# Two attention layers and two feed-forward layers in one kernel: the last expert's rows by a product, the fold earlier, three batches with the plain context

## The chip, the cores and the metric

One core of one Trainium2 chip runs the whole program. The metric is the device time of one execution in microseconds, the median of the runs. Everything is in float32 except a few small bfloat16 helpers.

## The reference

`x` has 8 batches of 112 rows and 256 columns, the context 8 batches of 375 rows. Four residual stages follow one another:

```python
x = x + L0_xattn(layernorm(x), ctx)      # 16 heads
x = x + L0_moe(layernorm(x))             # 8 experts of 112 slots each, top 1
x = x + L1_xattn(layernorm(x), ctx)      # one head of width 256, scores / sqrt(16)
x = x + L1_ffn(layernorm(x))             # 1024 hidden, plus rank-one terms from rows of x
```

In the expert stage each row goes to the expert with the largest gate; its slot is the expert's number times 112 plus its rank among the rows of that expert, and rows past 112 are dropped. The row gets back its gate times the expert's output at its slot. In the second attention the value is `v = ctx @ Wv + bv`, and the result `softmax(...) @ v`. Because the probabilities of a row sum to one, `softmax @ (ctx @ Wv) = (softmax @ ctx) @ Wv`, and `bv` is added to the residual separately.

## The kernel before

The tensor engine's program is written out in the order in which it runs; the other engines follow by semaphores. Each engine runs its own list strictly in order. Products go to one of 8 banks of PSUM; `open_bank` makes the tensor engine wait until every earlier product of that bank has been read (`drained`), `full` makes the reader wait until it is written (`filled`). Where it does not matter which bank is used, `next_bank` goes round a list by one counter; `CTX_BANKS` is (2, 3, 6, 7).

1. **First attention** (to about 172 us). `PIPE` and, for the last batches, `LAST` give for each step `(i, u)` the small pieces that run beside the scores: C1 to C6 and D5, D6 are the output projection, the norm and the router of one batch; ND, NM the row maxima. "CV" with a number means so many chunks of `project_context`: one chunk is 125 rows of the context times `Wv` of the second attention, two matmuls of 256 columns, and the scalar engine copies it to `ctxV` (L964). There are 24 chunks (3 for each batch); they depend on nothing that is late, so they are put wherever the tensor engine would wait.
2. **Experts** (L645 to L685). GpSimd has scattered each batch's rows to DRAM by slot (L1417), and SP has loaded them back by expert. `expert_rows` transposes the rows of an expert (bank 6 or 7), `expert_up` makes the 1024 hidden values, `expert_down` the output (bank 4 or 5). VectorE adds `b2` to the output (L1253) and SP stores it to `eo_dram` (L1535); the buffers are `eo0` and `cc` in turn. 7 chunks stand before the first expert, one behind the first up product.
3. **Behind the experts** (L690 to L711). The tensor engine makes the fold `Wq Wk^T` of the second attention (`WQK`, L695, 4 matmuls of 256 columns), a chunk, the products of the biases (`WQKB`, L704 and L707), and four chunks. Meanwhile GpSimd waits until the outputs of all 8 experts are in DRAM, and gathers each batch's rows from there (L1442, 8 indirect DMAs). VectorE's `combine` (L1268) waits for the gathered rows of a batch, adds gate times rows to the residual (L1271) and takes the moments for the norm (L1105 to L1107); GpSimd makes the inverse root (L1372), VectorE normalises (L1111).
4. **Second attention** (loop over `i`, `attend(stage, b)` with `b = i - stage`). Stage 0 transposes the normalised rows (XT3), 1 multiplies by the fold (QK), 2 makes the scores (S1), 3 transposes the probabilities (PT), 4 multiplies them by `ctxV` (O1), 5 transposes the rows for the last stage (XT4). The two last chunks stand at `i` = 0 and `i` = 1 (`CTX_IN_SECOND`). VectorE in each `i`: the norms, the combines (batches 1 and 2 at `i` = 0, then `i` + 2), then stages 4 and 2.
5. **Last feed-forward**, from `i` = 9 on, to the end at 352.8 us.

Of the kernel before, what the change touches and what calls it, by code (L numbers as in the profile page):

```python
# [6 lines left out]
ALU = mybir.AluOpType  # L7
# [105 lines left out]
CTX_AFTER_FIRST_UP = 1  # L113
CTX_BEHIND_FOLD = 1
CTX_IN_SECOND = {0: 1, 1: 1}
CTX_BANKS = (2, 3, 6, 7)

# [68 lines left out]
def build(nc, A):  # L186
    out = A["out"]
    with ExitStack() as ctx:
# [60 lines left out]
        wv_at1 = w_in[:, 0]  # L249

        unread = sb("unread", [1, 1])
        vones = [sb(f"vones{n}", [P, NKC, H, VW]) for n in range(2)]
        ctxU = sb("ctxU", [P, 4 * S])
        cc = sb("cc", [S, D])
# [22 lines left out]
        idx_get = sb("idx_get", [S, NB], I32)  # L277

# [9 lines left out]
        wqk = cut(late, DT * D).rearrange("p (k e) -> p k e", k=DT)  # L288
# [3 lines left out]
        tq = [cut(late, 1) for _ in range(2)]  # L292

# [44 lines left out]
        ld_wv_at1 = sem("loaded_at1_wv")  # L338
        ld_ring = [sem(f"loaded_expert{n}") for n in range(RING)]
# [47 lines left out]
        def _(pe):  # L387
# [161 lines left out]
            def project_context(n, banks):  # L549

                for _ in range(n):
                    t = chunks_done[0]
# [11 lines left out]
            def post(stage, b):  # L564
                if stage == "CV":
                    project_context(b, spare)
                elif stage in ("P0", "P1", "P2"):
                    weighted(b, int(stage[1]))
                elif stage in ("V0", "V1", "V2"):
# [105 lines left out]
            for e in range(E + 1):  # L675
# [7 lines left out]
                if e == 0:  # L683
                    project_context(CTX_AFTER_FIRST_UP, (5,))
# [6 lines left out]
            pe.wait_ge(ld["at1w"], 32)  # L691
            o = open_bank("WQK", 0)
            for m in range(DT):
                for k in range(DT):
                    mm = pe.matmul(o[:, m * D:(m + 1) * D], w_at1[:, 0, k, m * P:(m + 1) * P], w_at1[:, 1, k, :],  # L695
                                   start=k == 0, stop=k == DT - 1)
            mm.then_inc(filled[0], 1)
            project_context(CTX_BEHIND_FOLD, CTX_BANKS)
# [11 lines left out]

            project_context(NB * NKC - chunks_done[0] - sum(CTX_IN_SECOND.values()), CTX_BANKS)  # L711

            def attend(stage, b):
# [26 lines left out]
                elif stage == 3:  # L740
# [5 lines left out]
                    mm.then_inc(filled[4], 1)  # L746
                elif stage == 4:
# [4 lines left out]
                    for c in range(NKC):  # L752
                        mm = pe.matmul(o[0:S, 0:D], pT1[s][0:KC, c, :], ctxV[0:KC, NKC * b + c, :],  # L753
                                       start=c == 0, stop=c == NKC - 1)
                    mm.then_inc(filled[6], 1)
# [61 lines left out]
            for i in range(FFN_STEPS):  # L817
                for stage in (4, 2, 3, 1, 0):
                    if 0 <= i - stage < NB:
                        attend(stage, i - stage)  # L820
# [810 lines left out]
```

## Time and profile before

| | |
|---|---|
| median of 3 runs (lowest to highest) | 355.02 us (355.02 to 355.38) |
| the profiled execution's own time | 354.55 us |
| its span, first to last instruction | 352.8 us |
| PE (tensor engine, matmul) busy | 341.8 us, 97% |
| PEld (its weight loads, beside the matmuls) | 261.5 us, 74% |
| DVE (VectorE) / ACT (ScalarE) / POOL (GpSimd) busy | 189.2 / 146.1 / 57.7 us |
| granted TensorE clock | 1.000 |

The engine times overlap, so they are no sum. Each float32 matmul stands in the trace as two LDWEIGHTS and two MATMUL instructions; "x8" at L695 are the 4 matmuls of the fold. A "start us" is counted from the span's start. In the timeline the bracket behind a row says how long the engine had stood idle and who released it; the durations of matmuls in it overlap a little, so the pace of a row of matmuls is read from the chain, where they are laid end to end.

### The profile page before, as it was taken

What the parts mean: (1) busy time and instruction counts of PE and PEld (TensorE: products, weight loads), DVE (VectorE), ACT (ScalarE), POOL (GpSimd) and SP (SyncE); (2) the same over time, 40 slices, a digit from 0 to 9 for tenths busy, and PEclk for the clock granted to TensorE, in tenths of its full rate; (3) what the DMA queues carried; (4) which work ended last, traced back from release to release, by engine and by line L of the source; (5) the groups of instructions that cost most, each with busy time, mean ns of one, the idle gap of its engine ahead of it and who ended that gap; (6) DMA issues with size and microseconds to landing.
All of it is one profiled execution on the core that took longest, in us unless ns stands there. A gap on an engine that the chain in (4) does not pass through costs nothing.

```text
span 352.8 us, 7953 instructions
## 1 busy us (share of the span) xinstructions
PE 341.8 (97%) x3128; PEld 261.5 (74%) x3128; DVE 189.2 (54%) x591; ACT 146.1 (41%) x340; POOL 57.7 (16%) x95
## 2 busy tenths in 40 slices
PE   7999999999999999997999999999899999999996
PEld 6546566666666666665889998988688889797875
DVE  4674668857675867755721121212987667351500
ACT  2437353646365545554431221112446675332400
POOL 3200204101010010101200000134865211200000
DMA  8984150700001000062074999811110101101000
GB/s 234 336 260 159 32 208 5 251 4 13 3 9 37 2 15 3 16 238 76 20 216 142 323 339 331 238 40 52 39 28 3 44 16 54 55 27 52 29 26 26
DMA packets 24884, 35.28 MB, mean 100 GB/s; under 512 B 2608, under 2 KB 21408, under 8 KB 24736
## 3 DMA queue, kind: packets, MB, share of 16 engines
q1 hardware_dynamic: 22160, 31.73, 28.0%
q0 software_dynamic: 768, 1.84, 1.7%
q10 hardware_dynamic: 1920, 1.21, 1.3%
q8 instruction: 25, 0.41, 0.5%
q14 instruction: 11, 0.09, 0.1%
HBM read 31.06 MB, written 3.72 MB: 99 GB/s over the span
## 4 chain that ended last, share of the span: by engine, by line
PE 85%; DVE 6%; issue 3%; ACT 3%; POOL 2%; DMA 1%; DVEq 0%; POOLq 0%; ACTq 0%; SPq 0%
PE ps L661 8%; PE ps L806 8%; PE ps L671 8%; PE ps L784 7%; PE ps L424 6%; PE ps L497 6%; PE ps L517 5%; PE ps L452 5%; PE ps L560 4%; PE ps L538 4%; PE ps L737 3%; PE ps L512 2%; PE ps L608 2%; PE ps L753 2%; PE ps L415 2%
## 5 line engine op out<-in xcount | busy, mean ns | idle before, releaser
L1143 DVE TENSOR_REDUCE mneg<-ps 112x2 f32<-112x750 f32 x64 | 56.9, 932 | 19.2 <-PE ps L497 19.2
L1372 POOL TENSOR_TENSOR rstd<-veps,neghalf 112x1 f32<-112x1 f32 x32 | 18.6, 582 | 98.3 <-DVE veps L1107 97.4
L924 ACT ACTIVATE heads<-ps 125x896 f32<-125x896 f32 x34 | 29.3, 915 | 12.5 <-PE ps L517 12.5
L497 PE MATMUL ps<-heads 32*112 32x375 f32 x256 | 30.8, 519 | 0.1
L661 PEld LDWEIGHTS ps<-xT,ring 128*128 128x128 f32 x256 | 29.8, 192 | 1.1 <-ACT xT L877 0.7
L661 PE MATMUL ps<-xT,ring 128*128 128x112 f32 x256 | 29.9, 275 | 0.4 <-ACT xT L877 0.4
L806 PE MATMUL ps<-heads,ring 128*112 128x256 f32 x128 | 28.8, 382 | 0.0
L671 PE MATMUL ps<-ring,heads 128*112 128x256 f32 x128 | 28.8, 379 | 0.0
L806 PEld LDWEIGHTS ps<-heads,ring 128*112 128x112 f32 x128 | 22.4, 177 | 6.1 <-issue 1.4
L452 PE MATMUL ps<-w_in,ctxT 128*125 128x256 f32 x96 | 26.5, 402 | 0.0
L517 PE MATMUL ps<-heads 32*125 32x224 f32 x384 | 25.6, 354 | 0.0
L671 PEld LDWEIGHTS ps<-ring,heads 128*112 128x112 f32 x128 | 22.1, 177 | 4.4
L784 PE MATMUL ps<-xT,heads 128*128 128x224 f32 x128 | 24.9, 353 | 0.0
L1260 DVE TENSOR_SCALAR heads<-ps,b1col 128x112 f32<-128x112 f32 x32 | 8.6, 327 | 29.3 <-PE ps L661 29.3
L784 PEld LDWEIGHTS ps<-xT,heads 128*128 128x128 f32 x128 | 24.0, 190 | 0.1
L424 PE MATMUL ps<-ctxT,w_in 128*128 128x375 f32 x64 | 23.7, 492 | 0.2 <-ACT vones L907 0.2
L560 PE MATMUL ps<-w_in,ctxT 128*125 128x256 f32 x96 | 23.4, 385 | 0.0
L452 PEld LDWEIGHTS ps<-w_in,ctxT 128*125 128x125 f32 x96 | 16.2, 187 | 8.9 <-issue 6.3
L981 ACT ACTIVATE heads<-ps,b1col 128x112 f32<-128x112 f32 x32 | 8.7, 354 | 33.1 <-PE ps L661 33.1
L1312 DVE SCALAR_TENSOR_TENSOR ring<-ring,xT,ps 128x112 f32<-128x112 f32 x64 | 16.9, 326 | 8.5 <-PE ps L784 8.5
L1051 ACT ACTIVATE ring<-ring,fb1col 128x224 f32<-128x224 f32 x32 | 13.6, 474 | 19.0 <-DVEq L1317 18.9
L1417 POOL DMA_INDIRECT expert_in_dram<-xn,idx_put x8 | 8.0, 996 | 77.9 <-DVE idx_put L1219 77.9
(150 smaller groups left out, 552.8 us busy)
## 6 DMA issues: line engine op xcount, KB each, us to landing
ring<-in_L_ffn_W SPq DMA_DIRECT2D x16, 1024.0 KB, 6.3
ctxT<-in_ctxT SPq DMA_DIRECT2D x8, 375.0 KB, 11.5
heads<-in_L_ffn_W SPq DMA_DIRECT2D x2, 1024.0 KB, 9.4
ring<-x_by_odd_rows_dram SPq DMA_DIRECT2D x4, 448.0 KB, 3.7
ring<-in_mask SPq DMA_DIRECT2D x1, 1312.5 KB, 7.1
expert_in_dram<-eo SPq DMA_DIRECT2D x1, 896.0 KB, 11.0
b2row<-in_L_ffn_b SPq DMA_DIRECT2D x8, 112.0 KB, 7.4
out_dram<-ring SPq DMA_DIRECT2D x8, 112.0 KB, 1.9
```

The costliest lines, as they stand in the source:

```text
L424: mm = pe.matmul(o[:, 0:S2], w_in[:, 1, k, m * P:(m + 1) * P], ctxT[:, k, b * S2:(b + 1) * S2], start=k == 0, stop=k == DT - 1)
L452: mm = pe.matmul(o[0:KC, 0:D], ctxT[:, k, b * S2 + c * KC:b * S2 + (c + 1) * KC], w_in[:, 2, k, :], start=k == 0, stop=k == DT - 1)
L497: mm = pe.matmul(tile(("MX", b, g), j)[0:S, 0:S2], qz[rows, m, a, b * S:(b + 1) * S], kt[b % 3][rows, m, :], start=True, stop=True)
L517: mm = pe.matmul(tile(key, j)[0:KC, x * QW:(x + 1) * QW].rearrange("p (a q) -> p a q", a=2), kt[b % 3][rows, m, c * KC:(c + 1) * KC], qz[r ...
L560: mm = pe.matmul(o[0:KC, 0:D], ctxT[:, k, b * S2 + c * KC:b * S2 + (c + 1) * KC], wv_at1[:, k, :], start=k == 0, stop=k == DT - 1)
L661: mm = pe.matmul(o[:, f * S:(f + 1) * S], w1e[e % RING][:, k, ft * P:(ft + 1) * P], xT[:, k, e * S:(e + 1) * S], start=k == 0, stop=k == D ...
L671: mm = pe.matmul(o[0:S, 0:D], hid[e % 2][:, ft, :], w2e[e % RING][:, ft, :], start=ft == 0, stop=ft == FT - 1)
L784: mm = pe.matmul(o[:, f * 2 * S:(f + 1) * 2 * S], w1f[:, k, ft * P:(ft + 1) * P], xT[:, k, 2 * p * S:2 * (p + 1) * S], start=k == 0, stop= ...
L806: pe.matmul(o[0:S, 0:D], gT[p % 2][:, ft, x * S:(x + 1) * S], w2f[:, ft, :], start=ft == 0, stop=False)
L924: act.activation(weights(b, step)[0:KC, js.start:js.stop, :], o[0:KC, :, 0:2 * QW], ACT.Exp, scale=DK ** -0.5).then_inc(free, 1)
L1143: v.tensor_reduce(mneg[:, b % 2, PAIRS * g + js.start:PAIRS * g + js.stop], o[0:S, :, 0:S2], AX.X, ALU.max, negate=True).then_inc(free, 1)
L1372: g.tensor_tensor(rstd[:, b:b + 1], veps[:, b:b + 1], neghalf[:, b:b + 1], ALU.pow)\
```

## The change

Three things, all in one step.

**The last expert's rows by a product.** For batches 0 to 2 (`BY_PRODUCT`) VectorE builds a 112 by 112 matrix of ones and zeros from the rows' slots (`at_slot`: row's slot equals 784 + column). The tensor engine transposes it behind the rows of experts 1, 2 and 3, ScalarE copies it (`from_slot`), and behind the last expert's output three products `ER` (banks 4, 6, 7) pick the rows from the output still on chip (`cc`). The gathers of these batches read only experts 0 to 6 (rows of the last expert get index 0 and gate 0) and wait only for those stores. `combine` of these batches adds twice: the gathered rows, then the product. The gathers of batches 3 to 7 are issued one by one behind the roots of batches 0 to 4.

**The fold ahead of the experts.** `WQK` becomes a stage "FW" at step (8, 3), in place of two of the three chunks there; its result goes to a weight buffer that is free by then.

**Three batches weigh the plain context.** For batches 3, 4, 5 (`RAW`) the chunks are not made; SP loads their context rows as they are into `ctxV` (1.1 MB, behind the weights of expert 2). Stage 4 then makes `(softmax @ ctx)` transposed (PC, bank 7, 6 matmuls of 112 columns), ScalarE copies it (`pcT`) and at the end of the same `i` a product with `Wv` (WV, 2 matmuls of 256 columns) fills O1. VectorE takes stage 2 ahead of stage 4 for them. Of 24 chunks 15 are left: 9 go away, namely the one at (6, 1), two at (8, 3), the one behind the first up product, and all five behind the experts. Those at `i` = 0 and 1 stay.

```diff
-    (6, 1): [("C2", 5), ("CV", 1), ("C6", 4), ("D6", 4)],
+    (6, 1): [("C2", 5), ("C6", 4), ("D6", 4)],
-    (8, 3): [("CV", 3), ("L2", 7), ("D6", 6)],
+    (8, 3): [("FW", 0), ("CV", 1), ("L2", 7), ("D6", 6)],
...
@@ tensor engine
+                elif stage == "FW":
+                    pe.wait_ge(ld["at1w"], 32)
+                    n = next_bank(spare)
+                    o = open_bank("WQK", n)
+                    ... (the four matmuls that stood behind the experts)
...
             def expert_rows(e):
                 n = 6 + e % 2
                 pe.wait_ge(xe_loaded[PART_OF[e]], 16)
-                transpose_x("XE", e, n)
+                o = open_bank(("XE", e), n)
+                for k in range(DT):
+                    mm = pe.transpose(o[:, k * S:(k + 1) * S], xn[:, e, k * P:(k + 1) * P], ident[0:S, 0:S])
+                if 1 <= e <= BY_PRODUCT:
+                    pe.wait_ge(at_slot_ready, e)
+                    mm = pe.transpose(o[0:S, DT * S:(DT + 1) * S], at_slot[e - 1], ident[0:S, 0:S])
+                mm.then_inc(filled[n], 1)
...
-                if e == 0:
-                    project_context(CTX_AFTER_FIRST_UP, (5,))
...
-            (fold), project_context(CTX_BEHIND_FOLD, CTX_BANKS)
+            for b in range(BY_PRODUCT):
+                if b == 0:
+                    read(("DN", E - 1))
+                read(("XE", b + 1))
+                n = (4, 6, 7)[b]
+                pe.matmul(open_bank(("ER", b), n)[0:S, 0:D], from_slot[b], eo[(E - 1) % 2][:, :], start=True, stop=True)\
+                  .then_inc(filled[n], 1)
...
-            project_context(NB * NKC - chunks_done[0] - sum(CTX_IN_SECOND.values()), CTX_BANKS)
+            project_context(len(CTX_CHUNKS) - chunks_done[0] - sum(CTX_IN_SECOND.values()), CTX_BANKS)
...
+                elif stage == 4 and b in RAW:
+                    pe.wait_ge(ld_raw, 16)
+                    read(("PT", b))
+                    o = open_bank(("PC", b), 7)
+                    for m in range(DT):
+                        for c in range(NKC):
+                            mm = pe.matmul(o[:, m * S:(m + 1) * S], ctxV[0:KC, NKC * b + c, m * P:(m + 1) * P],
+                                           pT1[s][0:KC, c, :], start=c == 0, stop=c == NKC - 1)
+                    mm.then_inc(filled[7], 1)
...
+                elif stage == "WV":
+                    read(("PC", b))
+                    o = open_bank(("O1", b), 6)
+                    for k in range(DT):
+                        mm = pe.matmul(o[0:S, 0:D], pcT[:, k, :], wv_at1[:, k, :], start=k == 0, stop=k == DT - 1)
...
@@ VectorE
+            v.wait_ge(slot_row_ready, 1)
+            step(v.tensor_copy(slot_of[:, :], idx_get[:, 0:BY_PRODUCT]))
+            step(v.tensor_scalar(in_others[:, :], slot_of[:, :], float(LAST_SLOT), None, ALU.is_lt))
+            v.tensor_tensor(gate_others[:, :], gate[:, 0:BY_PRODUCT], in_others[:, :], ALU.mult)
+            v.tensor_tensor(idx_others[:, :], slot_of[:, :], in_others[:, :], ALU.mult).then_inc(others_ready, 1)
+            for b in range(BY_PRODUCT):
+                v.tensor_scalar(at_slot[b], slot_row, slot_of[:, b:b + 1], None, ALU.is_equal).then_inc(at_slot_ready, 1)
...
-                step(v.scalar_tensor_tensor(xres[:, b, :], xn[:, b, :], gate[:, b:b + 1], xres[:, b, :],
+                weight = gate_others if b < BY_PRODUCT else gate
+                step(v.scalar_tensor_tensor(xres[:, b, :], xn[:, b, :], weight[:, b:b + 1], xres[:, b, :],
                                             ALU.mult, ALU.add))
+                if b < BY_PRODUCT:
+                    o, free = full(("ER", b))
+                    v.scalar_tensor_tensor(xres[:, b, :], o[0:S, 0:D], gate[:, b:b + 1], xres[:, b, :],
+                                           ALU.mult, ALU.add).then_inc(free, 1)
+                    drained_by_me(("ER", b))
...
-                for stage in (4, 2):
+                for stage in (2, 4) if i - 4 in RAW else (4, 2):
...
@@ GpSimd
+            g.wait_ge(eo_stored[0], 16 * (E // 2))
+            g.wait_ge(eo_stored[1], 16 * (E // 2 - 1))
+            g.wait_ge(others_ready, 1)
+            for b in range(BY_PRODUCT):
+                gather(b, idx_others, LAST_SLOT)
+            for i in range(GATHER_AHEAD, NB + GATHER_AHEAD):
+                root(3, i - GATHER_AHEAD)
+                if i == GATHER_AHEAD:
+                    g.wait_ge(eo_stored[1], 16 * (E // 2))
+                if i + 1 < NB:
+                    gather(i + 1, idx_get, T)
...
@@ SP, behind the loads of experts 0 to 2
+            sp.dma_start(ctxV[0:KC, NKC * RAW[0]:NKC * (RAW[-1] + 1), :],
+                         A["ctx"][:, NKC * RAW[0]:NKC * (RAW[-1] + 1), :]).then_inc(ld_raw, 16)
```

## Rows read from the trace of the kernel before

**Rows 1.** Chain that ended last, in order of time: start us, us, what.

```profile
173.15 6.16 PE ps L560 x28
...
188.60 0.19 PE ps L415 x2
188.79 3.46 PE ps L671 x16
...
261.52 0.89 PE ps L727 x8
...
262.97 1.30 PE ps L753 x6
```

**Rows 2.** Timeline, 138 to 147: start us, us, engine line op out<-in, count [idle before <-releaser].

```profile
138.98 1.78 DVE L1143 TENSOR_REDUCE mneg<-ps 112x2 f32<-112x750 f32 x2 [0.24 <-PE ps L497]
...
142.50 0.42 DVE L1183 TENSOR_TENSOR xres<-ps,xres 112x256 f32<-112x256 f32 x1 [0.40 <-PE ps L608]
...
146.30 0.11 PEld L584 LDWEIGHTS ps<-identb,mpieces 112*128 112x128 bf16 x2 [0.28 <-DVE mpieces L1157]
```

**Rows 3.** DMA issues by line: KB each, median us to landing.

```profile
heads<-in_L_xattn_Wk SPq DMA_DIRECT2D x1, 256.0 KB, 3.8
```

**Rows 4.** Timeline, 159 to 170, the fold's weights and the chunks of (8, 3).

```profile
159.29 0.47 SPq L1516 DMA_DIRECT2D heads<-in_L_xattn_Wk  x1
...
167.43 2.83 PE L560 MATMUL ps<-w_in,ctxT 128*125 128x256 f32 x12
```

**Rows 5.** Timeline, 183.8 to 189, behind the first expert's up product.

```profile
183.81 0.36 PE L415 MATMUL ps<-ident,xn 112*128 112x112 f32 x2
...
184.20 0.36 ACT L877 ACTIVATE xT<-ps 128x224 f32<-128x224 f32 x1 [0.89 <-PE ps L415]
...
184.88 3.72 PE L661 MATMUL ps<-xT,ring 128*128 128x112 f32 x32
```

**Rows 6.** Busy time by stretch, with counts (x), granted clock (PEclk), DMA share, GB/s.

```profile
180.00:238.80 58.80, 58.66 (x403) 53.65 (x404) 11.55 (x40) 11.67 (x41) 3.90 (x8) 1.00 0.74 238
238.80:251.80 13.00, 11.94 (x72) 10.11 (x70) 6.45 (x20) 4.94 (x15) 7.55 (x9) 1.00 0.18 53
...
262.00:285.00 23.00, 23.00 (x155) 18.44 (x155) 17.20 (x54) 13.93 (x45) 8.76 (x15) 1.00 0.08 23
```

**Rows 7.** Timeline, 235 to 252, behind the experts.

```profile
235.83 0.31 SPq L1535 DMA_DIRECT2D expert_out_dram<-eo  x1
...
238.79 0.42 DVE L1253 TENSOR_TENSOR cc<-ps,b2row 112x256 f32<-112x256 f32 x1 [3.03 <-PE ps L671]
239.29 0.30 SPq L1535 DMA_DIRECT2D expert_out_dram<-cc  x1
...
241.18 1.84 PE L704 MATMUL ps<-bcol,heads 128*128 128x1 f32 x16
...
241.93 0.99 POOL L1442 DMA_INDIRECT xn<-expert_out_dram,idx_get  x1 [9.61 <-DMA expert_out_dram<-cc]
...
244.66 0.48 DVE L1271 SCALAR_TENSOR_TENSOR xres<-xn,gate,xres 112x256 f32<-112x256 f32 x1 [5.44 <-DMA xn<-expert_out_dram,idx_get]
...
246.70 0.41 DVE L1111 TENSOR_SCALAR xn<-xres,mv,rstd 112x256 f32<-112x256 f32 x1 [0.69 <-POOL rstd L1372]
...
247.03 0.48 DVE L1271 SCALAR_TENSOR_TENSOR xres<-xn,gate,xres 112x256 f32<-112x256 f32 x1
...
247.17 0.41 PE L415 MATMUL ps<-ident,xn 112*128 112x112 f32 x2 [0.20 <-DVE xn L1111]
...
248.29 0.47 DVE L1271 SCALAR_TENSOR_TENSOR xres<-xn,gate,xres 112x256 f32<-112x256 f32 x1
...
249.55 0.40 DVE L1111 TENSOR_SCALAR xn<-xres,mv,rstd 112x256 f32<-112x256 f32 x1
...
250.26 1.04 PE L560 MATMUL ps<-w_in,ctxT 128*125 128x256 f32 x4
...
251.86 1.49 PE L737 MATMUL ps<-ctxT,ring 128*112 128x375 f32 x4 [0.56 <-ACT ctxV L964]
```

More of the change, by code:

```diff
@@ L112 @@
 CTX_BEFORE_EXPERTS = 7
-CTX_AFTER_FIRST_UP = 1
-CTX_BEHIND_FOLD = 1
 CTX_IN_SECOND = {0: 1, 1: 1}
 CTX_BANKS = (2, 3, 6, 7)
+RAW = (3, 4, 5)
+CTX_CHUNKS = [NKC * b + c for b in range(NB) if b not in RAW for c in range(NKC)]
+BY_PRODUCT = 3
+LAST_SLOT = (E - 1) * CAP
 ROW_PARTS = ((0, 1), (1, 2), (2, 4), (4, E))
@@ L253, in build @@
         ctxU = sb("ctxU", [P, 4 * S])
+        slot_row = vones[0][0:S, 0, :, :].rearrange("p h w -> p (h w)")[:, 0:S]
+        at_slot = [vones[1][0:S, b, :, :].rearrange("p h w -> p (h w)")[:, 0:S] for b in range(BY_PRODUCT)]
+        from_slot = [ctxU[0:S, b * S:(b + 1) * S] for b in range(BY_PRODUCT)]
         cc = sb("cc", [S, D])
@@ L971, in _ @@
                         copy_context_values(b)
+                    elif stage == "FW":
+                        o, free = full("WQK")
+                        act.activation(wqk, o[:, 0:DT * D].rearrange("p (k e) -> p k e", k=DT), ACT.Copy)\
+                           .then_inc(free, 1)
                     elif stage in ("V0", "V1", "V2", "K0", "K1", "QX", "Q0", "Q1", "U", "C2", "C4", "D5"):
@@ L991, in _ @@
                 if e + 1 < E:
+                    if e < BY_PRODUCT:
+                        o, _ = full(("XE", e + 1))
+                        act.activation(from_slot[e], o[0:S, DT * S:(DT + 1) * S], ACT.Copy)
                     copy_xT("XE", e + 1)
-                if e == 0:
-                    copy_context_values(CTX_AFTER_FIRST_UP)
             def attend(stage, b):
@@ L1024, in attend @@
                                    ACT.Copy).then_inc(free, 1)
+                elif stage == 4:
+                    o, free = full(("PC", b))
+                    if b - 1 in RAW:
+                        act.wait_ge(*filled_at(("O1", b - 1)))
+                    act.activation(pcT[:, :, :], o[:, 0:DT * S].rearrange("p (k s) -> p k s", k=DT), ACT.Copy)\
+                       .then_inc(free, 1)
                 elif stage == 5:
@@ L1066, in _ @@
             act.activation(bqbk[0:S, :], o[0:S, 2 * DT:2 * DT + 1], ACT.Copy).then_inc(free, 1)
-            copy_context_values(NB * NKC - chunks_done[0] - sum(CTX_IN_SECOND.values()))
+            copy_context_values(len(CTX_CHUNKS) - chunks_done[0] - sum(CTX_IN_SECOND.values()))
             for i in range(FFN_STEPS):
+                if i - 4 in RAW:
+                    attend(4, i - 4)
                 for stage in (3, 1, 2, 0):
@@ L1434, in _, with gather @@
                  .then_inc(mask_ready, 1)
-            for n in range(2):
-                g.wait_ge(eo_stored[n], 16 * E // 2)
             def plus(b, r, s):
                 g.tensor_tensor(xres[:, b, :], xres[:, b, :], browL1[:, r, :], ALU.add).then_inc(s, 1)
-            for i in range(NB + GATHER_AHEAD):
-                if i < NB:
-                    g.indirect_dma_start(out=xn[:, i, :], out_offset=None, in_=eo_dram,
-                                         in_offset=bass.IndirectOffsetOnAxis(ap=idx_get[:, i:i + 1], axis=0))\
-                     .then_inc(got_rows[i], 16)
-                if i >= GATHER_AHEAD:
-                    root(3, i - GATHER_AHEAD)
+            def gather(b, idx, slots):
+                g.indirect_dma_start(out=xn[:, b, :], out_offset=None, in_=eo_dram[0:slots],
+                                     in_offset=bass.IndirectOffsetOnAxis(ap=idx[:, b:b + 1], axis=0))\
+                 .then_inc(got_rows[b], 16)
+            g.wait_ge(eo_stored[0], 16 * (E // 2))
[9 more added lines that the diff above has]
+                    gather(i + 1, idx_get, T)
                 if i == GATHER_AHEAD:
```

39 lines of the change are left out of this document (24 added, 15 removed).

## The prediction

> **What bounds the kernel now.** Read the busy shares first: the tensor engine is at 97% (341.8 of 352.8 us), the others at half or less, so time goes where its work or its few waits go. Then the busy time by stretch, to see where those waits lie: none to speak of over the experts (58.66 of 58.80 us) and none from 262 to 285, but 1.06 us of 13.00 behind the experts [rows 6]. The chain of waits gives the pace of each kind of product [rows 1]: a product of 256 columns costs 0.22 us an instruction (6.16/28, 3.46/16, 1.30/6), one of 112 columns 0.111 (0.89/8). The timeline behind the experts shows what is late there and what the chunks cover: the round trip of the last expert's rows [rows 7]. The clock is granted in full in all these stretches, 1.00 [rows 6], its upper level, 2.4 GHz.
>
> **Work on the tensor engine, by itself.** Nine chunks go: 9 x 4 x 0.22 = 7.9 us. New are three ER products (3 x 2 x 0.22 = 1.3), three transposes (half of the 0.19 of a pair, 0.3 together [rows 1]), and in each of the three batches with plain context PC, 12 instructions at 0.111 = 1.33, plus WV, 4 at 0.22 = 0.87, in place of O1's 1.30: 0.9 more, 2.7 in all. That is 3.6 us less work. Whoever stops here forecasts 351. But the chunks were fillers: the question is for each whether it stood beside a wait.
>
> **1. The chunk at (6, 1).** It costs 0.88. The scores behind it move up by that, but VectorE is in a double row maximum from 138.98 to 140.76 whatever the tensor engine does [rows 2], then has the router of batch 4 (about 1.3 us), so its sum at 142.50 can come only some 0.4 earlier; and the tensor engine already waits for VectorE at 146.30 [rows 2]. I take 0.45 of the 0.88, bounds 0 and 0.88.
>
> **2. The fold for two chunks at (8, 3).** Four matmuls of 256 columns each way, 8 instructions at 0.22 [rows 1]. Nothing changes as long as its weights are there: the second half is issued at 159.29 and takes 3.8 us [rows 3]; the place is at 167.43 [rows 4]. Zero; ScalarE has one large copy instead of two small.
>
> **3. The chunk behind the first up product.** It covered expert 1's rows on their way out of PSUM. Transposes start at 183.81, the copy ends at 184.56, the next up product starts at 184.88 [rows 5]. Without the chunk that path itself is the time, and it grows by the third transpose (0.1) and the copy of `from_slot` ahead of the rows on ScalarE (nothing to 0.36, the row of a copy twice as wide [rows 5]; I take 0.27, as it is fixed cost more than width). The up product starts near 185.0: 0.1 later, not 0.88 earlier. The other two transposes add 0.1 each, their copies lie under 3.46 us of down product [rows 1]. Together +0.3 (0.1 to 0.5). So the last down product ends within 0.2 us of where it does now: -0.15.
>
> **4. Behind the experts, in the times of the old trace.** VectorE has the last output in `cc` at 239.21 (238.79 + 0.42). ER then runs to 240.6, the tensor engine having waited 0.5; the bias products (20 instructions that load 128 or 112 columns, at 0.111 as in rows 1 is 2.2; the sixteen of L704 take 1.84 [rows 7]) to 242.8. What comes next needs batch 0 normalised. Its gathered rows depend on expert 6's store: issued at 235.83; the last store took 2.64 from issue to the gather's start (239.29 to 241.93) and the gather 2.73 to its use (241.93 to 244.66) [rows 7], so they are there at 241.2. The old path from use to transpose is 2.51 (244.66 to 247.17); the second addition puts 0.52 to it (a row of 0.48 and its wait). XT3 of batch 0 is at 244.2, 2.9 earlier, with 1.4 idle before it.
>
> Now the combines of batches 1 and 2. They start at 247.03 and 248.29 today, 1.26 apart, and batch 1 is normalised at 249.55 [rows 7]. With two additions each is 1.78: starts at 244.1 and 245.9, the second addition of batch 2 ends at 246.9, batch 1 is normalised at 247.65, 1.9 earlier. Of the 2.9 gained 1.0 is given back.
>
> And the tensor engine waits for more than that. The chunk at `i` = 0 goes to the bank the counter gives. Eight calls of `next_bank` fewer (nine chunks less, the fold more) are two full rounds of four banks, so the two last chunks fall in banks 7 and 2 as now; that bank 2 is the last one's is seen, since S1 of batch 0 (bank 2) waits for ScalarE's copy of a chunk at 251.86 [rows 7]. Bank 7 now holds ER of batch 2 and is free when VectorE has added it: 246.9. So the chunk, and QK of batch 0 and all behind it, stand from 245 to 246.9. Chunk to 247.8, QK (8 + 4 small instructions, 1.35) to 249.15, XT3 of batch 1 to 249.4, last chunk, and by the 1.60 from that to S1 (250.26 to 251.86 [rows 7]) S1 at 251.0. **The stretch gains 0.85, though 4.8 us of work went out of it.** Lower bound of the gain 0.3 (rows or the store 0.5 later), upper 1.9 if the bank didn't hold. The gathers of batches 3 and 4 are no limit: issued behind the roots at about 243.9 and 246.8, there 2.73 later, needed at 247.8 and 249.8.
>
> The Trainium skill (DMA: Bandwidth & Descriptors, Anatomy of one DMA) gives a transfer 2.0 us plus its bytes over 436 GB/s; an estimate by it for 112 KB is 2.26 us each for store and gather, so batch 0's rows 0.85 us sooner than by the rows here. By that the stretch would gain 1.7 instead of 0.85. This case's 2.64 and 2.73 include the wait for the sequencer, and I go by them.
>
> **5. The three batches with plain context.** In `i` = 7, 8, 9 the tensor engine never waits (23.00 of 23.00 us, 262 to 285 [rows 6]), so the 0.9 each is paid in full: +2.7. PC's copy lies under S1 and PT, 1.6 us at least. O1 comes at the end of `i`: additions, moments, root and norm, the 2.51 us of rows 7, are through before XT4, which stands behind some 5 us of products in the next `i`. Bounds: 0.095 an instruction if the pace went by columns (112/256 of 0.22) gives +2.1; a VectorE that falls behind some 0.3 for each `i`, +3.6 (it is busy 17.20 of 23.00 us there [rows 6], 3.2 in an `i` of 4.3 that becomes 5.2).
>
> The Trainium skill (TensorE: Matmul & The Clock Gate, LDWEIGHTS) has a weight load go by its columns at 1.2 a ns, 107 ns for 128. PC loads 128 columns for every 112 it streams, which speaks against this part of the change; 0.111 from the rows agrees with it, 0.095 does not.
>
> **6. The rest.** The mask of slots is seven small operations on VectorE behind the router and one iota on GpSimd, near 176 us, where VectorE has only memsets to do until the first expert's hidden values: nothing; without that cover about 1.5. The 1.1 MB of context are loaded behind expert 2's weights, long before use at 270, and the next entry of SP's queue waits for a much later product: nothing. The three early gathers stand on GpSimd ahead of the first root, until 242.0, which it needs at 243.1.
>
> **Sum.** -0.45 + 0.3 - 0.85 + 2.7 = +1.7 on the profiled execution's 354.55 us: 356.25. The median of the runs lies 0.47 above that execution, so the forecast is 355.02 + 1.7 = 356.7 us, slower by 0.5%.
>
> **The rivals.**
> - *The bank is no wait* (the chunk at `i` = 0 starts at once): the norm of batch 1 alone decides, the stretch gains 1.9, the sum is +0.65: 355.7. For it: the norm path is sound either way. Against it: the count of calls, and bank 2 in the trace.
> - *Faster: the round trip was all.* Batch 0's rows are in `xn` before the last down product ends, the transposes follow the bias products at 242.7, 4.5 earlier than 247.17, and the tensor engine keeps that lead. Then -0.15 - 4.5 + 2.7 = -1.95: 353.1. For it: the wait for the store is what the old trace shows. Against it: 2.64 + 2.73 behind 235.83, and the doubled combines. It decides from the point where S1 of batch 0 comes less than 10.5 us after the last output is ready for VectorE (13.07 now, 238.79 to 251.86).
> - *Slower still: VectorE lags with the plain batches.* It does the norms, then the scores, then O1; if each `i` of 7 to 9 stretches by 0.5, +3.2 in all: 358.2. For it: O1's chain moves to the end of `i`, by the 3.9 us of products now ahead of it. Against it: the 2 us in an `i` that VectorE has free.
> - *The fold waits, or the gather chain of the later batches does*: the same +3, with less behind it.
>
> **Chances.** Forecast 0.50 (its own range 355.9 to 357.5), bank no wait 0.17, faster 0.15, slower still 0.13, others 0.05. 0.2%, 0.7 us, is what a measurement of this kernel can tell from no change: faster means below 354.3, slower above 355.7. Faster has the third case, 0.15; the second stands on the upper edge and goes half to either side, which with a low tail of the forecast gives the same 0.19; slower 0.66. The range leaves out most of the case at 353.1: 354.2 to 358.2.
>
> **What would show it.** Right: no idle at the fold in (8, 3); about 0.8 us idle ahead of the second up product; 0.5 idle ahead of ER, 1.4 ahead of the first XT3, then a wait of 2 us of a chunk (L560's line) released by VectorE; S1 of batch 0 some 12.2 us behind the last output; PC 1.33 and WV 0.87 in each of three `i` without idle. Wrong: a chunk at `i` = 0 that starts at once, an S1 within 10.5 us, a PC below 1.2 us, idle between S1 of batch 3 and the first layer.

## The result and the profile after

The changed kernel takes 367.96 us (median of 4 runs, 366.83 to 368.85) against 355.02: slower by 3.45%, ratio 1.0345 (1.0311 to 1.0378). The forecast was 356.7. Of the 13 us the prediction has 1.7.

The first lines of the page, of the profiled execution after: the span, the tensor engine, and a line that the page before does not have, because there the clock was full throughout: PEclk, the granted clock in tenths.

```profile
span 367.1 us, 7978 instructions
...
PE 349.6 (95%) x3131; PEld 266.3 (73%) x3131; DVE 193.0 (53%) x601; ACT 144.2 (39%) x337; POOL 58.2 (16%) x96
...
PEclk9999999999999999999999999975698999999999
```

The tensor engine has less to do, as forecast, and is busy for longer: 349.6 us against 341.8. The busy time by stretch (columns as in rows 6: busy and count of PE, PEld, DVE, ACT, POOL, then granted clock) says where:

```profile
238.80:251.80 13.00, 10.21 (x50) 8.82 (x49) 9.71 (x27) 1.64 (x8) 9.30 (x12) 0.64 0.21 62
251.80:258.00 6.20, 5.63 (x16) 3.61 (x15) 1.28 (x4) 0.71 (x3) 3.66 (x5) 0.50 0.14 37
258.00:262.00 4.00, 3.63 (x12) 2.34 (x12) 1.51 (x6) 1.58 (x6) 1.27 (x2) 0.50 0.01 4
262.00:285.00 23.00, 21.37 (x130) 17.60 (x130) 14.54 (x44) 10.57 (x34) 7.12 (x11) 0.91 0.01 2
```

Behind the experts the granted clock is 0.64, then 0.50, which is the lower of its two levels, 1.2 GHz; before it was 1.00 in the same stretch, with 11.94 of 13.00 us busy [rows 6]. By single stretches of time, the same view:

```profile
241.00:242.00 1.00, 1.00 (x11) 1.00 (x10) 0.96 (x2) 0.00 (x0) 0.75 (x1) 1.00 0.41 122
242.00:243.00 1.00, 1.00 (x9) 1.00 (x8) 0.77 (x4) 0.00 (x0) 0.04 (x1) 0.71 0.38 112
243.00:246.00 3.00, 1.45 (x7) 1.02 (x6) 2.30 (x7) 0.59 (x3) 1.73 (x3) 0.50 0.13 37
262.00:263.00 1.00, 1.00 (x5) 0.71 (x5) 0.42 (x1) 0.00 (x0) 0.00 (x0) 0.55 0.00 0
...
280.00:283.00 3.00, 3.00 (x12) 2.38 (x11) 0.00 (x0) 0.36 (x1) 0.00 (x0) 0.50 0.03 8
283.00:284.00 1.00, 1.00 (x5) 0.67 (x4) 0.00 (x0) 0.00 (x0) 0.00 (x0) 0.81 0.01 2
```

It falls at about 242.4 and rises at 262.9, and falls a second time from 280.0 to 283.4. The timeline behind the experts, which answers to rows 7:

```profile
239.10 0.43 DVE L1317 TENSOR_TENSOR cc<-ps,b2row 112x256 f32<-112x256 f32 x1 [3.03 <-PE ps L705]
...
239.59 1.55 PE L728 MATMUL ps<-cc,ctxU 112*112 112x256 f32 x6 [0.52 <-DVE cc L1317]
...
240.97 2.10 PE L735 MATMUL ps<-bcol,heads 128*128 128x1 f32 x16
241.00 0.48 DVE L1336 SCALAR_TENSOR_TENSOR xres<-xn,gate_others,xres 112x256 f32<-112x256 f32 x1 [1.47 <-DMA xn<-expert_out_dram,idx_others]
...
244.03 0.64 PE L433 MATMUL ps<-ident,xn 112*128 112x112 f32 x2 [0.22 <-DVE xn L1168]
...
246.18 0.48 DVE L1340 SCALAR_TENSOR_TENSOR xres<-ps,gate,xres 112x256 f32<-112x256 f32 x1
...
246.72 2.07 PE L578 MATMUL ps<-w_in,ctxT 128*125 128x256 f32 x4 [2.06 <-DVE xres L1340]
...
253.80 2.81 PE L768 MATMUL ps<-ctxT,ring 128*112 128x375 f32 x4 [0.56 <-ACT ctxV L1012]
```

Read it against the prediction: ER starts 0.52 us after the wait for the last output (forecast 0.5), batch 0's rows are used at 241.00 (241.2), its XT3 is at 244.03 (244.2), the chunk of `i` = 0 starts at 246.72, released by VectorE's second addition of batch 2 after 2.06 us (246.9). (Two errors cancel in this: the last output came 0.3 later, and the store of expert 6's rows took 2.12 from issue to the gather, 236.15 to 238.27, where 2.64 was taken.) Only S1 of batch 0 is at 253.80 and not at 251.0: a chunk takes 2.07 where it took 0.9, and QK and the transposes take about twice as long too. The chain of waits was forecast rightly; the clock at which it ran was not.

The second part of the loss is at `i` = 7 to 9. Chain of waits, first after (columns as in rows 1), then the two lines of before that bound the same stretch:

```profile
277.13 0.32 PE ps L761 x4
...
279.51 2.46 PE ps L784 x12
281.97 2.02 PE ps L768 x4
...
299.44 6.08 PE ps L830 x32
```

```profile
271.25 0.30 PE ps L730 x4
...
285.17 6.08 PE ps L784 x32
```

From the end of the last QK instructions of `i` = 6 to the first layer it is 13.62 us before (271.55 to 285.17) and 21.99 after (277.45 to 299.44). The list of waits names the cause (engine and line, waited for, us in total, times, longest):

```profile
PE ps L784 <- ACT xT L925: 3.3, 3, 1.6
```

PC (L784) waits three times for ScalarE's copy of `xT`. It opens bank 7, and XT4 of an earlier batch, transposed at the end of the `i` before, is still in it until ScalarE, which has QK, the exponential and XT3 first, comes to its copy.

**The 14.3 us of span, stretch by stretch** (length in us, before and after; a row begins where the one above it ends, with the last output's addition on VectorE as the first border):

| stretch | before | after | difference | forecast |
|---|---|---|---|---|
| start to the last output's addition | 238.79 | 239.10 | 0.31 | -0.15 |
| to S1 of batch 0 | 13.07 | 14.70 | 1.63 | -0.85 |
| to the end of QK in `i` = 6 | 19.69 | 23.65 | 3.96 | 0 |
| to the first layer | 13.62 | 21.99 | 8.37 | +2.7 |
| to the end of the span | 67.63 | 67.66 | 0.03 | 0 |

### The profile page after: what moved, and what is told of

It is laid out like the page before. It is cut to its first block, busy times and chain, and to the rows that moved or that the text cites. A ratio compares the mean times of both kernels' runs of the same rounds, so it can differ in the third digit from the quotient of the medians.

```text
span 367.1 us, 7978 instructions
## 1 busy us (share of the span) xinstructions
PE 349.6 (95%) x3131; PEld 266.3 (73%) x3131; DVE 193.0 (53%) x601; ACT 144.2 (39%) x337; POOL 58.2 (16%) x96
## 4 chain that ended last, share of the span: by engine, by line
PE 82%; DVE 5%; ACT 5%; DMA 4%; issue 2%; POOL 0%; ACTq 0%; DVEq 0%; SPq 0%; POOLq 0%
PE ps L695 8%; PE ps L852 8%; PE ps L830 7%; PE ps L705 7%; PE ps L515 6%; PE ps L535 5%; PE ps L442 5%; PE ps L470 5%; PE ps L556 4%; PE ps L578 4%; PE ps L768 4%; DMA w_in<-in_L_xattn_Wv 3%; PE ps L758 2%; PE ps L530 2%; PE ps L635 2%
## 5 line engine op out<-in xcount | busy, mean ns | idle before, releaser
L470 PE MATMUL ps<-w_in,ctxT 128*125 128x256 f32 x96 | 26.6, 403 | 0.1
L1406 DVE TENSOR_TENSOR ring<-ps,xres 112x256 f32<-112x256 f32 x8 | 3.4, 424 | 29.5 <-PE ps L860 29.4
```

Source lines behind the costliest of these rows:

```text
L470: mm = pe.matmul(o[0:KC, 0:D], ctxT[:, k, b * S2 + c * KC:b * S2 + (c + 1) * KC], w_in[:, 2, k, :], start=k == 0, stop=k == DT - 1)
```

## The experiments

Each was run beside the kernel before on the same chip; the changed kernel itself was measured only in the run above. The median of the kernel before moved there between 355.5 and 355.8.

Executions of one kernel differ by some 3 us and more, so medians are given with their lowest execution. The mean granted clock is on record for every execution, and most of the spread goes with it. The kernel before has, in 72 executions beside these experiments, 39 with a mean clock of 0.999 or more (354.4 to 356.2 us), 21 with 0.994 or 0.995 (355.4 to 356.2) and 12 with 0.985 or 0.986 (358.6 to 359.5). So that kernel, too, is at the lower clock for some us in almost half of its executions, though not in the one that was profiled ahead of the prediction. Where its falls lie is not known, as no such execution of it was profiled.

**Theory:** two things cost, both outside the work that was counted. The clock falls where the tensor engine is given little to stream (a wait, or products of one column), and PC waits for a bank. **Rivals:** only waits lower the clock; ER or the products themselves cost more than was counted for them; PC waits for its own input.

### PC in another bank

```diff
-                    o = open_bank(("PC", b), 7)
+                    pc = 3 - s
+                    o = open_bank(("PC", b), pc)
```

> The changed kernel with PC in the score bank that is free (3 - b mod 2) instead of bank 7. Theory (PC waits for ScalarE's copy of XT4 in bank 7, 1.6, 1.0 and 0.7 us, and the first of these waits lets the clock fall from 280 to 283.8): no wait of L784's line for xT is left, the granted clock stays 1.00 from 264 to 300, and the time falls by 3.3 us of waits and about 1.9 us of half clock, to 362 to 363.5. The fall from 242 to 263 stays. Rival (PC waits for its own input, the copied probabilities): within 1 us of 368.

362.14 us (lowest 358.58, 4 runs). The waits are gone and so is the second fall. Chain of waits, one plain batch in each `i`:

```profile
277.18 0.30 PE ps L761 x4
...
277.92 1.34 PE ps L785 x12
...
282.29 0.87 PE ps L801 x4
...
293.85 6.08 PE ps L831 x32
```

The stretch is 16.37 us (277.48 to 293.85) against 13.62: +2.75, and the forecast's 2.7 with its terms (PC 1.33, WV 0.87) stands. So bank 7 cost 5.6 of the 8.4: 3.3 as waits, 1.9 as half clock behind the first of them (PC 2.46 for 1.34, S1 2.02 for 1.26), and 0.4 because the two PC behind the other waits took 1.56 each. The fall behind the experts stays, from 245.7 to 262.7.

### Work that nobody reads

Four products the size of a chunk, into bank 3, whose result is not used: one ahead of ER, one behind the bias products, two ahead of the chunk at `i` = 0; then the same with PC in its own bank.

```diff
+            fill(1)
             for b in range(BY_PRODUCT):
...
+            fill(1)
...
+                if i == 0:
+                    fill(2)
                 project_context(CTX_IN_SECOND.get(i, 0), CTX_BANKS)
```

> The changed kernel with four products more that nobody reads, each the size of a chunk (bank 3): one ahead of ER, one behind the bias products, two ahead of the chunk at i = 0. No wait is taken away. Theory (the clock fell at 242.3 because work of 256 columns was taken out around the bias products, and stayed low through the 2 us wait for bank 7): with more work the kernel is faster; clock 1.00 from 239 to 264, S1 of batch 0 some 12.3 us behind the last output's addition instead of 14.7, S1 to QK of i = 6 in 19.7 us instead of 23.7, the time about 361.5. Rival (the clock falls for another reason, the engine's power or the products of 112 rows): clock low in the same place, time 368 to 370.

> Both edits: the four unread products and PC in its own bank. Theory: full clock throughout, and what is left is the change's work and the wait for bank 7: 355.9 to 357.5, which is what the prediction had without a word on the clock. Rival: if the two falls of the clock are not all, the sum of the two gains falls short and the time stays above 359.

362.87 us (4 runs) and 356.92 us (10 runs), lowest 362.55 and 356.40. Each is 5 us below its partner without the unread products (367.96 and 362.14): more work is faster. The chunk at `i` = 0 is still held back by bank 7, and the engine has products to do meanwhile. The profile of the first by stretch:

```profile
239.00:242.00 3.00, 3.00 (x20) 2.64 (x18) 1.22 (x3) 0.00 (x0) 2.23 (x3) 1.00 0.42 112
242.00:244.00 2.00, 2.00 (x17) 1.94 (x17) 1.21 (x5) 0.23 (x2) 0.68 (x2) 0.96 0.20 62
244.00:247.00 3.00, 3.00 (x9) 2.26 (x9) 2.79 (x9) 0.36 (x1) 1.73 (x3) 0.50 0.14 38
247.00:250.00 3.00, 3.00 (x21) 2.73 (x20) 2.79 (x10) 0.38 (x1) 2.79 (x3) 0.95 0.13 38
```

The fall is still there, against the expectation, but it lasts some 3.4 us (243.8 to 247.3) instead of 20. S1 of batch 0 is 12.51 us behind the last output's addition, and from there to the end of QK in `i` = 6 it is 19.71 us, as in the kernel before (19.69). So the second and third rows of the table were the clock's doing.

With both edits the kernel is where the prediction had it, 356.92 for 356.7, and 0.23% above the kernel before (ratio 1.0023, 0.9979 to 1.0068). Seven of its ten executions have a mean clock of 1.000, and their median is 356.66 against 354.78 for the six of the kernel before in the same company with 0.999 or more: 1.9 us, where 1.7 was forecast. Its profiled execution, at 360.02, is not one of them. There the clock falls twice: behind the experts, from 246.8 to 250.2, and in the router stage, from 164.9 to 171.7, which the change barely touches:

```profile
164.00:171.00 7.00, 6.30 (x21) 4.61 (x21) 3.46 (x18) 1.31 (x6) 0.16 (x1) 0.56 0.05 16
...
247.00:252.00 5.00, 5.00 (x21) 4.11 (x19) 4.62 (x15) 0.59 (x2) 3.53 (x5) 0.68 0.16 45
```

The fall in the router stage makes everything behind it 2.9 us later (the chunk behind the fold starts at 172.29, in the changed kernel at 169.38). So the two falls of the changed kernel and the bank account for the 11 us that were not forecast.

### The chunk's bank alone, and both banks

```diff
-                project_context(CTX_IN_SECOND.get(i, 0), CTX_BANKS)
+                project_context(CTX_IN_SECOND.get(i, 0), (5,) if i == 0 else CTX_BANKS)
```

> The changed kernel with the chunk at i = 0 in bank 5, which is free, instead of bank 7, which ER of batch 2 holds. Theory (the clock is down before this wait begins, but the wait keeps it down longer): no wait of 2 us ahead of the chunk, S1 of batch 0 earlier by 1 to 2 us, clock still 0.50 from about 242 on; the time 1 to 3 us below the changed kernel's 368. Rival (the wait is the cause of the fall): clock 1.00 throughout 239 to 264 and the time 6 us or more lower.

> The changed kernel with both bank waits taken away (PC in a free score bank, the chunk at i = 0 in bank 5) and no work added. Theory (thin work behind the experts suffices for the fall): the clock is still 0.50 for some 15 us from somewhere between 242 and 248 on, the time 358.5 to 361. Rival (only the waits for banks brought the clock down): clock 1.00 and about 356.

363.31 us (lowest 359.49; 362.26 without the longest of the four, 365.21) with the chunk's bank alone, and 358.30 (lowest 355.38, 10 runs) with both. S1 of batch 0 is 11.77 and 10.71 us behind the last output's addition, and 14.70 in the changed kernel. Two stretches of the first:

```profile
242.00:246.00 4.00, 3.14 (x22) 2.85 (x23) 3.07 (x11) 0.98 (x4) 1.68 (x2) 0.92 0.18 47
246.00:254.00 8.00, 7.15 (x22) 4.95 (x22) 5.62 (x16) 1.49 (x5) 7.22 (x9) 0.50 0.17 49
```

Three stretches of the second:

```profile
239.00:244.00 5.00, 4.48 (x21) 3.38 (x20) 0.64 (x2) 0.00 (x0) 2.00 (x3) 1.00 0.22 63
244.00:252.00 8.00, 7.13 (x45) 6.53 (x44) 6.63 (x20) 1.72 (x8) 5.09 (x6) 0.79 0.21 58
252.00:264.00 12.00, 10.84 (x69) 8.39 (x68) 11.07 (x31) 4.79 (x18) 9.73 (x13) 1.00 0.11 32
```

Without a wait for bank 7 the clock still falls behind the experts, later and for less long: from 246.9 to 250.3, some 3.4 us where 15 were expected. So the waits for that bank are not needed for a fall. That they lengthen it is likely (20.5 us in the changed kernel, 10.2 without the first wait, 3.4 without both) but rests on one profiled execution of each kernel, and with the first wait still there a_pc_bank has 17.1.

The time of the second has two clusters, four executions from 355.4 to 355.7 and six from 358.2 to 359.6. What parts them is not the fall behind the experts. None of the ten has a mean clock above 0.995; the four have 0.994 or 0.995, which works out to some 3.5 us at half clock, as much as that fall, and the six have 0.981 to 0.986. The profiled one is one of the six (358.42), and 6.8 of its 10.2 us at half clock lie in the router stage, from 164.9 to 171.7:

```profile
166.00:168.00 2.00, 1.31 (x5) 0.78 (x4) 0.43 (x4) 1.25 (x5) 0.00 (x0) 0.50 0.00 0
168.00:170.00 2.00, 2.00 (x8) 1.46 (x7) 0.49 (x2) 0.00 (x0) 0.00 (x0) 0.50 0.00 0
```

Its last output is added at 242.25 and not at 239.10: the 3 us between the clusters. So with the banks mended the change is worth nothing either way in the lower four, a short fall included. The 3 us more of the others belong, as far as the profiled one shows, to a stage that the change barely touches; the 12 high executions of the kernel before have much the same mean clock. Against c_fill_pc_bank, where seven of ten executions have no fall, here every one has some half clock: the added work keeps the clock up, the mended banks alone do not.

### One part at a time

Without the plain context (24 chunks again, seven behind the experts, in banks 2, 3 and 5):

```diff
-    (6, 1): [("C2", 5), ("C6", 4), ("D6", 4)],
+    (6, 1): [("C2", 5), ("CV", 1), ("C6", 4), ("D6", 4)],
...
-CTX_BANKS = (2, 3, 6, 7)
-
-RAW = (3, 4, 5)
+CTX_BANKS = (2, 3, 5)
+
+RAW = ()
...
+                if e == 0:
+                    project_context(1, (5,))
```

> The change without its third part: all 24 chunks are made again (the chunk at (6, 1) and the one behind the first up product are back, seven stand behind the experts, in banks 2, 3 and 5), no batch weighs the plain context; the product and the early fold stay. Theory (the clock falls because the tensor engine's work behind the experts was thinned out): clock 1.00 from 239 to 264, and the time is that of the work: S1 of batch 0 some 13.8 us behind the last output against 13.07, 0.3 for the transposes, so about 1 us above the kernel before, 356. Rival (ER or the bias products behind it bring the clock down): 0.50 for some us behind 242 and 360 or more.

357.42 us (lowest 355.42, 7 runs), ratio 1.0052 (1.0023 to 1.0081). The profiled execution, at 355.86, has a clock of 1.00 throughout, and S1 of batch 0 is 13.56 us behind the last output's addition (13.8 expected):

```profile
239.00:252.00 13.00, 12.48 (x76) 10.74 (x74) 9.60 (x26) 3.55 (x11) 9.31 (x12) 1.00 0.22 63
```

So ER and the bias products behind it do not bring the clock down where chunks surround them. But this holds for three of the seven executions (355.4 to 356.0); the other four have mean clocks of 0.990 to 0.995 and take 357.4 to 359.1. Falls are rarer here and shorter, not gone.

Without the product (the old gather, no ER; PC in a free bank):

```diff
-            for b in range(BY_PRODUCT):
-                ... (ER)
-            for b in range(BY_PRODUCT):
-                gather(b, idx_others, LAST_SLOT)
+            for i in range(NB + GATHER_AHEAD):
+                if i < NB:
+                    gather(i, idx_get, T)
...
```

> The change without its first part: the old gather of all batches from DRAM, no ER; the fold stays early, three batches weigh the plain context (PC in a free score bank). Behind the experts only the bias products are left for the tensor engine, which then waits about 5 us for batch 0. Theory (missing work lowers the clock): clock 0.50 from about 244 to 262 as in the changed kernel, the time about 1 us above that of the changed kernel with PC in its own bank, which took 362.1. Rival (the doubled additions and the bank of ER are what costs): 358 or less.

360.50 us (lowest 358.54), where 1 us above 362.1 was expected. The executions of the two kernels overlap (358.54 to 363.72 here, 358.58 to 363.24 with the product), so all that is shown is that the product gains nothing that can be told in this company.

```profile
241.00:247.00 6.00, 0.00 (x0) 0.00 (x0) 1.54 (x5) 0.13 (x2) 3.58 (x5) 0.52 0.20 57
247.00:252.00 5.00, 4.83 (x22) 4.42 (x23) 4.53 (x15) 0.97 (x4) 4.12 (x6) 0.56 0.16 46
252.00:256.00 4.00, 3.44 (x21) 2.49 (x20) 2.33 (x6) 1.15 (x5) 3.77 (x6) 1.00 0.12 32
```

In the wait of 6.3 us (not one matmul from 241 to 247) the clock is down nearly from its start, at 241.2, and it is back at 251.4, where it was expected to stay down to 262.

### Light work without a wait

The kernel before, with its one-column bias products three times:

```diff
-            for side in range(2):
+            for side in [0, 1] * 3:
```

> The kernel before, with its sixteen one-column bias products (L704) made three times (the last result is the one used): 32 instructions more, 3.6 us, in which the tensor engine loads weights and streams one column each, and never waits. Theory (the clock falls where little is streamed, be the engine busy or not): clock 0.50 for some us from about 244 on in most runs, the time 6 us or more above the kernel before. Rival (only waiting counts): clock 1.00, and 2.5 to 3.6 us above, since the wait for batch 0 was 0.2 us only.

361.96 us (lowest 361.11), 6.3 above the kernel before for 3.6 us of instructions.

```profile
241.00:244.50 3.50, 3.50 (x31) 3.42 (x29) 0.00 (x0) 0.94 (x2) 1.82 (x2) 1.00 0.11 32
244.50:248.00 3.50, 3.50 (x23) 3.50 (x22) 2.07 (x7) 0.00 (x0) 2.31 (x4) 0.65 0.26 74
248.00:252.00 4.00, 4.00 (x14) 3.33 (x14) 3.72 (x13) 0.62 (x3) 3.29 (x5) 0.50 0.20 56
```

The trace has the tensor engine busy without a gap from 237.7 on, and at 245.5, behind 3.9 us of one-column products, the clock goes to 0.50 until 252.2. Being busy, as the trace counts it, did not keep the clock. This decides against the rival that only waits count. All four executions have a mean clock of 0.990 or less.

### Towards a version that gains

One plain batch (4), two batches by product, chunks back at (6, 1) and behind the first up product, one ahead of ER and three behind the bias products, all in free banks:

```diff
-RAW = (3, 4, 5)
+RAW = (4,)
-BY_PRODUCT = 3
+BY_PRODUCT = 2
...
+            project_context(1, (2,))
             for b in range(BY_PRODUCT):
...
-                project_context(CTX_IN_SECOND.get(i, 0), CTX_BANKS)
+                project_context(CTX_IN_SECOND.get(i, 0), {0: (5,), 1: (4,)}.get(i))
...
+            g.wait_ge(eo_stored[1], 16 * (E // 2))
+            gather(2, idx_get, T)
```

> A version that keeps what pays by these runs: two batches by product, one (batch 4) with the plain context and PC in a free score bank, the chunks back at (6, 1) and behind the first up product, one chunk ahead of ER and three behind the bias products, the chunks at i = 0 and 1 in free banks 5 and 4. Theory: no wait over 0.6 us, clock 1.00, S1 of batch 0 some 10.5 us behind the last output (13.07 before), one batch's 0.95 more later: 1.5 us below the kernel before, 353.5. Rival (the norms of batches 0 and 1 leave gaps in which the clock falls): 357 or more.

355.10 us (lowest 354.09, 7 runs), ratio 0.9986 (0.9945 to 1.0028): no difference that can be told, where 353.5 was expected. Its profiled execution, at 358.37, has two falls, one in the router stage (165.7 to 172.5) and one from 247.6 to about 251, a chunk and a half behind the bias products.

Then the bias products ahead of the last down product, with three batches by product:

```diff
+                if e == E:
+                    ... (the bias products, WQKB)
                 if e >= 1:
                     expert_down(e - 1)
```

> A version for a gain: three batches by product, one (batch 4) with the plain context, PC in a free score bank, the fold early, the chunks back at (6, 1) and behind the first up product, and the bias products moved from behind the experts to ahead of the last down product, where they take 2.2 us while expert 6's rows are stored and gathered; behind the last output stand ER with one chunk ahead of it, three chunks and those at i = 0 and 1, all in free banks. Theory: the rows of batch 0 are there when the last output is, S1 of batch 0 comes some 8.5 to 9 us behind the last output's addition (13.07 before) which itself is 2.5 later, products of 256 columns surround the stage and the clock stays 1.00 there: 353.5 to 354.5, 1 to 2 us below the kernel before on the same chip. Rival (the norms leave gaps, or the bias products lower the clock wherever they stand): a fall behind 240 and 357 or more.

356.76 us (lowest 355.23, 12 runs), ratio 1.002 (0.9983 to 1.0056), where 353.5 to 354.5 was expected. The half of the executions with a mean clock of 1.000 takes 355.2 to 356.1, so a fall is not all of the difference; what the rest is stays open. In the profiled execution S1 of batch 0 is 8.88 us behind the last output's addition, as expected (8.5 to 9), but the addition itself is at 243.53, 4.7 us later than before where 2.5 was expected. In this execution, at 357.58, the clock falls in the down product behind the bias products:

```profile
236.00:238.00 2.00, 2.00 (x20) 1.98 (x19) 0.42 (x1) 0.00 (x0) 0.00 (x0) 1.00 0.18 52
238.00:242.00 4.00, 4.00 (x13) 3.03 (x13) 0.00 (x0) 0.23 (x2) 2.58 (x3) 0.57 0.17 47
242.00:252.00 10.00, 9.30 (x52) 7.88 (x51) 6.82 (x20) 3.19 (x10) 4.48 (x6) 1.00 0.15 44
```

Then the bias products in three pieces, with a chunk behind each, and the unchanged version beside it on the same chip:

```diff
             for side in range(2):
                 ... (eight one-column instructions)
+                project_context(1, CTX_BANKS)
```

> The version with one plain batch and two by product (g_one_raw), its bias products no longer in one piece: eight of the one-column instructions, a chunk, the next eight, a chunk, the last four, a chunk. The work and its sum are the same. Theory (the clock falls where many of the light products stand together): fewer falls behind 246, the clock 1.00 from 239 to 264 in the profile, the median within 0.5 us of the undisturbed 354.1 to 354.5, 0.2% to 0.4% below the kernel before. Rival (the order of light and heavy products doesn't matter, only their share): falls as often as in g_one_raw, median 355 or more.

> The version g_one_raw on the same chip as k_spread, in five rounds, as its partner: its undisturbed executions at 354.1 to 354.5, falls of the clock in about half of them, median near 355.

354.10 us (353.64 to 356.76, 12 runs), ratio 0.9957 (0.9931 to 0.9983), **0.4% below the kernel before**; its partner in one piece 354.95 us, ratio 1.0004 (0.9970 to 1.0039), with executions up to 359.03. The two intervals overlap; only this one leaves out 1.

At full clock both gain: the executions with a mean clock of 0.999 or more have medians of 354.04 (11 of 12), 354.33 (7 of 12) and, for the kernel before, 355.03 (9 of 23). So the version itself is worth 0.7 to 1 us. What the order of the bias products adds is fewer executions with a fall, one of twelve against five, and with so few that can be chance. Besides, three of those five are at 358.1 to 359.0 with mean clocks of 0.985 or 0.986, which in the profiled execution of g_one_raw came in the larger part from the router stage, ahead of all that differs between the two.

By stretch, and on the timeline, the version in three pieces:

```profile
239.00:247.00 8.00, 8.00 (x51) 7.04 (x49) 5.22 (x15) 2.15 (x8) 4.67 (x7) 1.00 0.25 72
```

```profile
239.21 0.42 DVE L1324 TENSOR_TENSOR cc<-ps,b2row 112x256 f32<-112x256 f32 x1 [3.03 <-PE ps L705]
...
245.52 0.36 PE L433 MATMUL ps<-ident,xn 112*128 112x112 f32 x2
...
248.99 1.45 PE L771 MATMUL ps<-ctxT,ring 128*112 128x375 f32 x4
```

S1 of batch 0 is 9.78 us behind the last output's addition (239.21 to 248.99), against 13.07. In one piece it is 9.80.

## Why the prediction was wrong

**The step that failed first is a sentence of the opening part:** "The clock is granted in full in all these stretches". It was read as a property of the kernel. It was one of the profiled execution (33 of the 72 others show a lower mean clock) and of the work in these stretches. Part 4 took 4.8 us of products out of a stretch and left by its own count 0.5, 1.4 and 1.9 us of waits and 2.2 us of one-column products in it, and priced all that is left at the paces of rows 1. Measured: 0.50 of the clock from 242.4 to 262.9, so that the products cost double for 20 us. It accounts for 2.5 us in the second row of the table (1.63 against -0.85) and for the 3.96 of the third; b_fill, with the fall cut to 3.4 us, has 12.51 and 19.71 us there. The Trainium skill (TensorE: Matmul & The Clock Gate, Part 1) states that the engine's clock has a lower default that activity lifts, a rule that was in reach and speaks against this change; this trace agrees with it in kind, 0.50 behind a stretch with less work and 1.00 again at 262.9. A fall of the clock belonged among the rivals, with a price. Less work was slower for that reason, which c_fill_pc_bank and b_fill show by adding work.

**The second step that failed is in part 5:** "In `i` = 7, 8, 9 the tensor engine never waits (23.00 of 23.00 us, 262 to 285 [rows 6]), so the 0.9 each is paid in full". That row was of a kernel in which O1 went to bank 6, drained early. PC goes to bank 7, which XT4 fills last in each `i` and ScalarE empties last. The bank argument was made for the chunk and not for PC, though both stand in the same diff. It cost 3.3 us of waits and 2.3 behind them, 1.9 of these at half clock; a_pc_bank takes them away and finds 2.75 where 2.7 was forecast.

**What held.** Part 3: from expert 1's transposes to the second up product it is 1.05 us without the chunk (183.85 to 184.90) and 1.07 with it [rows 5], so nothing was gained there (forecast 0.1 lost, 0.8 idle, 0.60 measured). Part 2: no wait at the fold. Part 4's chain, each time within 0.3 us (in part by luck, as said above), and its wait for bank 7. Part 6, as far as the tensor engine's waits show. The sum without the clock and bank 7: +1.9 us at full clock in c_fill_pc_bank, four unread products included, for +1.7. The stretch to the last output came out 0.31 longer instead of 0.15 shorter, of which 0.38 is there already at 43 us, ahead of any edit. Behind (6, 1), at 143.4, the changed kernel is 0.13 later, so the chunk there gave 0.25 (forecast 0.45), and the tensor engine waits 0.46 for VectorE in its place. Expert 1's transposes are 0.04 later, and the experts took back 0.27 (0.3).

**The rivals.** None was what happened. "Slower still" had the right place, `i` = 7 to 9, and the wrong cause. The faster one had as its point an S1 within 10.5 us; k_spread gets there (9.78) with one plain batch instead of three, and is 0.4% below the kernel before. "The bank is no wait" did not happen, and h_banks shows what it would have given: with both banks mended the lower four executions take 355.4 to 355.7, as the kernel before (355.5), where that rival had 0.7 more.

**The size.** 11 us of the miss are the clock and bank 7 together, shown by c_fill_pc_bank. Where the fall starts is not fixed: at 242.4 in the changed kernel and at 245.7 in a_pc_bank, whose program is the same up to 277. What sets that was not settled, and so no single time can be forecast for such a kernel, only a spread.

## What to carry to other kernels

When a change thins out the tensor engine's work, ask of each stretch what the clock will be granted, not only what is left to do: work taken from beside a wait gains nothing, and may cost the clock for what follows. One profiled execution at full clock does not show that a kernel always has it; look at the mean clock of every execution. Filler products have a use of their own. Whether light work (one-column products, small transposes) is best laid between wide ones is suggested by k_spread and not shown. A new product's bank is part of its price: look who filled it last, and how far down the list of the engine that empties it.

## What the runs showed of the hardware

- The clock fell with the engine busy in every microsecond, in a stretch of one-column products (j_light, 3.50 of 3.50 us busy at 0.65, then 4.00 of 4.00 at 0.50).
- In the router stage it fell in three profiled executions (c_fill_pc_bank and h_banks, 164.9 to 171.7; g_one_raw, 165.7 to 172.5), behind a wait of 1.2 us, and in others not, the profiled one of the kernel before among them, which has the same wait (1.23 ahead of 163.06).
- Ahead of the fall at 280.0 (after) stands one wait of 1.6 us. In the profiled execution of the kernel before, four short waits, 1.06 us in 13, brought no fall.
- With dense products behind it the clock was back after 3.4 us (b_fill, 243.8 to 247.3; after, 280.0 to 283.4); with products that wait for each other it stayed low for 20 (after, 242.4 to 262.9).
- At half clock a chunk took 2.07 us (before 1.04), 12 PC instructions 2.46 (1.34 in a_pc_bank), the four of S1 2.81 (before 1.49): close to double. The stretches grew by less, as waits for other engines do not double: 20.5 us at half clock cost 6.4 (2.5 and 4.0).
